# One pool of eight PSUM banks, two turned parts of q and k, and a new order, in a post-norm decoder layer

## The reference

```python
x = layernorm(x + self_attention(x))   # 16 heads of 32; q, k rms-normalised over 512 and rotated; causal
x = layernorm(x + xattn(x, ctx, ctx))  # 8 "heads" of 16 rows: scores are 512x512 over the channels
x = layernorm(x + ffn(x))              # one 512x512 layer, inputs and weight rounded to fp8 blocks of 128

# self_attention
q, k, v = split(h @ Wqkv); q = rope(rmsnorm(q, qw)); k = rope(rmsnorm(k, kw))
o = softmax(causal(q @ k.T / sqrt(32))) @ v @ Wo
# xattn, per head: q, k, v are 16 x 512
ret = softmax(q.T @ k / 4) applied to v
```

## Time and profile before

| | before |
|---|---|
| median of 3 runs | 2888.91 us (2886.74 to 2889.34) |
| the profiled execution, its own time | 2883.74 us |
| its span, first to last instruction | 2882.0 us |
| mean granted clock of PE | 0.987 |
| PE / PEld busy | 2743.4 / 1341.7 us |
| DVE / ACT / POOL busy | 2623.3 / 2233.4 / 1609.2 us |
| DMA | 396.90 MB, 44.6% of 16 engines' span |

### The profile page before, as it was taken

The page is one execution under the profiler, slowest core; times in us unless marked ns, Lnnn a source line. Parts: engine busy times, 40 slices in busy tenths (PEclk is TensorE's granted clock), DMA queues, the critical chain, the costliest instruction groups (busy, mean ns, idle before and its releaser), DMA issues.

```text
span 2882.0 us, 77185 instructions
## 1 busy us (share of the span) xinstructions
PE 2743.4 (95%) x20769; PEld 1341.7 (47%) x20769; DVE 2623.3 (91%) x4038; ACT 2233.4 (77%) x4036; POOL 1609.2 (56%) x2257
## 2 busy tenths in 40 slices
PE   6799999999999999999999999999999999999986
PEld 4544444444444444444444444444444444444421
DVE  7689999999999999999999999999999999998995
ACT  4468788788788788887888887888888888778775
POOL 4446566556556556556556555555555555555543
PEclk8899999999999999999999999999999999999998
DMA  2244444444444444444444444444444444444561
GB/s 100 81 130 151 133 134 136 150 138 135 151 138 134 152 142 130 154 142 127 155 144 131 152 143 128 154 144 134 148 145 131 147 146 137 140 150 126 160 185 51
DMA packets 382299, 396.90 MB, mean 138 GB/s; under 512 B 84369, under 2 KB 313745, under 8 KB 382097
## 3 DMA queue, kind: packets, MB, share of 16 engines
q1 hardware_dynamic: 382096, 394.95, 44.6%
HBM read 208.68 MB, written 186.12 MB: 137 GB/s over the span
## 4 chain that ended last, share of the span: by engine, by line
PE 68%; DVE 19%; issue 7%; ACT 2%; POOL 1%; DMA 1%; SPq 1%; ACTq 0%; DVEq 0%; POOLq 0%
PE bank L1474 18%; PE st L1616 13%; PE pv L1628 12%; PE mx L1602 9%; DVE nm L1314 8%; PE bank L1525 3%; PE bank L1567 2%; DVE yc L1421 2%; PE bank L1467 2%; PE bank L1644 2%; PE bank L1539 2%; PE bank L1645 2%; DVE ropeA L1351 2%; PE bank L1570 1%; ACT pp L1138 1%
## 5 line engine op out<-in xcount | busy, mean ns | idle before, releaser
L1138 ACT ACTIVATE pp<-st 128x512 f32<-128x512 f32 x2048 | 1164.4, 596 | 233.3 <-PE st L1616 220.4
L1314 DVE TENSOR_REDUCE nm<-mx 128x2 f32<-128x1024 f32 x1024 | 1239.0, 1210 | 89.6 <-PE mx L1602 82.1
L1616 PE MATMUL st<-qst,kst 98*128 98x512 f16 x2048 | 738.0, 385 | 23.7 <-ACT pp L1138 21.8
L1628 PE MATMUL pv<-pp,vT 128*17 128x512 f32 x4096 | 537.8, 597 | 0.0
L1602 PE MATMUL mx<-kpair,qpair 64*128 64x512 bf16 x2048 | 399.5, 386 | 44.3 <-DVE nm L1314 36.9
L1474 PE MATMUL bank<-w_h,xT_h 128*128 128x512 f32 x768 | 417.5, 544 | 13.9 <-DVE xT_l L1343 8.1
L1616 PEld LDWEIGHTS st<-qst,kst 98*128 98x128 bf16 x2048 | 179.3, 97 | 401.8 <-issue 202.1
L1602 PEld LDWEIGHTS mx<-kpair,qpair 64*128 64x128 f16 x2048 | 99.0, 92 | 494.0 <-DVE nm L1314 275.6
L1062 POOL TENSOR_SCALAR_AFFINE_SELECT sm<-sm 128x512 f32<-128x512 f32 x256 | 162.8, 636 | 272.9 <-ACT sm L1181 271.3
L1474 PE MATMUL bank<-w_h,xT_l 128*128 128x512 f32 x768 | 307.7, 401 | 0.0
L1474 PE MATMUL bank<-w_l,xT_h 128*128 128x512 f32 x768 | 306.6, 399 | 0.0
(11 more groups left out here) (154 smaller groups left out, 5092.9 us busy)
## 6 DMA issues: line engine op xcount, KB each, us to landing
qst<-q_rows SPq DMA_DIRECT2D x128, 320.0 KB, 3.5
kst<-k_rows SPq DMA_DIRECT2D x128, 320.0 KB, 3.7
kpair<-k_pair_rows SPq DMA_DIRECT2D x256, 128.0 KB, 2.7
qpair<-q_pair_rows SPq DMA_DIRECT2D x256, 128.0 KB, 2.8
k_pair_rows<-kpl SPq DMA_DIRECT2D x64, 384.0 KB, 2.5
q_pair_rows<-qpl SPq DMA_DIRECT2D x64, 384.0 KB, 2.7
q_rows<-qpl SPq DMA_DIRECT2D x64, 384.0 KB, 3.8
k_rows<-kpl SPq DMA_DIRECT2D x64, 384.0 KB, 2.6
```

The lines of the kernel that those rows point to most:

```text
L1138: a.activation(pp[:, unit % 3, j, :], st[n % 2][:], ACT.Exp, scale=CROSS_SCALE).then_inc(st_free, 1)
L1314: v.tensor_reduce(cols, mx[:], AX.X, ALU.max, negate=True).then_inc(mx_free, 1)
L1616: t.matmul(st[n % 2][:], kst[:, h, i * P:(i + 1) * P], qst[:, h, :], start=True, stop=True).then_inc(st_full, 1)
L1628: last = t.matmul(pv[32 * j:32 * j + XD + 1, :], vT[b.i][:, i, GROUPS * j + g, :], pp[:, unit % 3, j, :], start=(i == 0), stop=(i == KC - 1))
```

## The change

PSUM becomes one tensor of eight banks. The table `BANK` gives a bank, and with it a place in that bank's sequence of turns, to every product, also to the 32 `cross_scores_T` (`SC_BANK`), the 16 pairs of `cross_scores` (`MX_BANK`), the two `cross_pv` groups and the turned weights of the fill. `before(name)` now waits on the semaphore of whichever turn held the bank last.

`qkn` has two slots, high and low, for heads i and i + 8 side by side. `part_high` writes one copy. `parts_T` has two steps instead of four, each of 8 transposes of 128 x 128. `self_stack` makes four copies of 64 rows x 1024, from the lower or the upper half of the turned rows, and a new step `copy_part` on SP copies 32 rows of 16 heads x 128 (128 KB) within `qs` and within `ks`; `self_scores:0` waits for both.

All five tables and the fill and drain lists are new. The weights are loaded, rounded and split in six halves, and the memsets of DVE on `qst` and `kst` become a step, `set_rows`, of the fill. The loop's first batch stays number 10.

```diff
-        qkn = [sb(f"qkn{i}", [P, NH, 3, HD], F16) for i in range(2)]
+        qkn = [sb(f"qkn{i}", [P, NH // 2, 2, 2, HD], F16) for i in range(2)]
...
-        st = [bank(f"st{i}") for i in range(2)]
-        pv = bank("pv")
-        mx = es.enter_context(nc.psum_tensor("mx", [P, 2, 512], F32))
-        banks = [bank(f"bank{i}") for i in range(3)]
-        d_w = [sem(f"d_w{i}") for i in range(3)]
+        psum = es.enter_context(nc.psum_tensor("psum", [P, 8, 512], F32))
+        banks = [psum[:, i, :] for i in range(8)]
...
-            ld_x:0@0 ld_kst:1@5 ld_x2r:0@6 ld_sh2:1@5 st_qpair:0@3 ld_qst:1@5 st_sh1:0@1
...
+            st_kpl:0@4 copy_part:0@0 st_qpair:0@2 copy_part:1@0 ld_cx:0@3 ld_qpair:0@3 st_qpl:0@2
...
-            "xT": 2, "tqk0": 0, "tqk1": 0, "tqk2": 1, "tqk3": 2, "q": 2, "k": 1, "v": 2, "s1m0": 1,
-            "s1m1": 0, "s1m2": 1, "s1m3": 1, "s1t0": 0, "s1t1": 0, "s1t2": 1, "s1t3": 1, "pvo": 2,
-            "pvs": 0, "wo": 2, "vT": 0, "xdT": 0, "ffn0": 1, "ffn1": 1, "ffn2": 1, "ffn3": 0}
+            "xT": 2, "tqk0": 6, "tqk1": 3, "q": 2, "k": 0, "v": 3, "s1m0": 3, "s1m1": 6, "s1m2": 7,
+            "s1m3": 3, "s1t0": 7, "s1t1": 4, "s1t2": 4, "s1t3": 3, "pvo": 5, "pvs": 0, "wo": 7, "vT": 5,
+            "pv0": 4, "pv1": 6, "xdT": 3, "ffn0": 6, "ffn1": 4, "ffn2": 1, "ffn3": 3,
+            "wt0": 5, "wt1": 0, "wt2": 4, "wt3": 1, "wpeak": 2}
+        SC_BANK = "47435167657737267272206423421703"
+        MX_BANK = "56 12 12 12 01 56 01 01 01 34 12 01 01 67 45 12"
+        BANK.update({f"sc{n}": int(i) for n, i in enumerate(SC_BANK)})
+        BANK.update({f"mx{q}{n}": int(sorted(pair)[i]) for n, pair in enumerate(MX_BANK.split())
+                     for i, q in enumerate("ab")})
...
+        OWN = {f"sc{n}": (st_free, N_SC, n + 1) for n in range(N_SC)}
+        OWN.update({f"mx{q}{n}": (mx_free, N_MX, n + 1) for n in range(N_MX) for q in "ab"})
+        OWN.update({f"pv{g}": (pv_free, GROUPS, g + 1) for g in range(GROUPS)})
...
+            turns, at = HELD[BANK[name]], AT[name, b.b]
+            if at == 0:
+                return Point(("free", BANK[name]), bank_free[BANK[name]], 0, b, 0)
+            turn, batch = turns[at - 1]
+            assert b.rnd is None or turns[AT[name, b.b + WRAP] - 1] == (turn, batch + WRAP)
+            if turn not in OWN:
+                return nth(turn, bank_free, "free", b, batch)
+            sem, per, n = OWN[turn]
+            return Point((turn[:2], 0), sem, per, b, batch * per + n)
...
+        def part(k, slot):
+            return qkn[k][:, :, :, slot, :].rearrange("p i e d -> p e i d")
+        def both(n):
+            low, high = BANK[f"mxa{n}"], BANK[f"mxb{n}"]
+            return psum[:, low:high + 1:high - low, :]
...
+            def copy_part(b, k):
+                sp.wait_ge(*freed(f"tqk{k}", b))
+                sp.sem_inc(passed_sp, 1)
+                rows = (qs, ks)[k]
+                sp.dma_start(rows[2 * HD:3 * HD], rows[HD * k:HD * (k + 1)]).then_inc(d_copied[k], 16)
...
-                g_.tensor_tensor(qkn[k][:, :, 2 - k, :], ropeA[:].rearrange("p h a d -> p h (a d)"),
-                                 qkn[k][:, :, 0, :], ALU.subtract).then_inc(s_part_l, 1)
+                g_.tensor_tensor(part(k, 1 - k), ropeA[:].rearrange("p (e i) a d -> p e i (a d)", e=2),
+                                 part(k, k), ALU.subtract).then_inc(s_part_l, 1)
...
-                a.activation(w_h[:, :, k * D:(k + 1) * D], pp[:, k], ACT.Copy).then_inc(u_cast, 1)
+                block, half = k // 2, slice(KC // 2 * (k % 2), KC // 2 * (k % 2 + 1))
+                a.activation(w_h[:, half, block * D:(block + 1) * D], pp[:, block, half], ACT.Copy).then_inc(u_cast, 1)
...
-                a.activation(pp[:, unit % 3, j, :], st[n % 2][:], ACT.Exp, scale=CROSS_SCALE).then_inc(st_free, 1)
+                a.activation(pp[:, unit % 3, j, :], at(f"sc{n}"), ACT.Exp, scale=CROSS_SCALE).then_inc(st_free, 1)
...
-                act.wait_ge(*full(f"tqk{2 * k + 1}", b, -1))
-                src = ropeA[:].rearrange("p h a d -> p h (a d)")
-                a.activation(qkn[k][:, :, 0, :], src, ACT.Copy)
-                a.activation(qkn[k][:, :, 1 + k, :], src, ACT.Copy).then_inc(s_part_h, 1)
+                act.wait_ge(*full(f"tqk{k}", b, -1))
+                a.activation(part(k, k), ropeA[:].rearrange("p (e i) a d -> p e i (a d)", e=2), ACT.Copy)\
+                 .then_inc(s_part_h, 1)
...
-                dst = (qs, ks)[i // 2][0:SROWS, 8 * (i % 2):8 * (i % 2) + 8, :]
-                a.activation(dst, at(f"tqk{i}")[0:SROWS, :].bitcast(F16).rearrange("p (h t) -> p h t", h=8), ACT.Copy)\
-                 .then_inc(bank_free[BANK[f"tqk{i}"]], 1)
+                half_rows = slice(2 * HD * (i % 2), 2 * HD * (i % 2 + 1))
+                dst = (qs, ks)[i // 2][0:2 * HD, 8 * (i % 2):8 * (i % 2) + 8, :]
+                copy = a.activation(dst, at(f"tqk{i // 2}")[half_rows, :].bitcast(F16)
+                                    .rearrange("p (h t) -> p h t", h=8), ACT.Copy)
+                if i % 2:
+                    copy.then_inc(bank_free[BANK[f"tqk{i // 2}"]], 1)
...
-            for rows, value in ((qst[64:XROWS, :, :], 0.0), (kst[64:XROWS, :, :], 0.0),
-                                (kst[XROWS:XROWS + 2, :, :], SHIFT_UNIT)):
+            for i in PV_BANKS:
+                v.memset(banks[i], 0.0).then_inc(u_zeroed, 1)
+            def set_rows(b, k):
+                rows, value = ((qst[64:XROWS, :, :], 0.0), (kst[64:XROWS, :, :], 0.0),
+                               (kst[XROWS:XROWS + 2, :, :], SHIFT_UNIT))[k]
+                if k == 2:
+                    dve.wait_ge(u_zeroed, len(PV_BANKS) + 2)
                 v.memset(rows, value).then_inc(u_zeroed, 1)
 
...
-                v.tensor_reduce(cols, mx[:], AX.X, ALU.max, negate=True).then_inc(mx_free, 1)
+                v.tensor_reduce(cols, both(n), AX.X, ALU.max, negate=True).then_inc(mx_free, 1)
...
-                for h in range(8):
-                    last = t.transpose(at(name)[0:SROWS, h * P // 2:(h + 1) * P // 2].bitcast(F16),
-                                       qkn[k][:, 8 * (i % 2) + h, :, :].rearrange("p g d -> p (g d)"), ident16[:])
+                for i in range(NH // 2):
+                    last = t.transpose(at(name)[:, i * P // 2:(i + 1) * P // 2].bitcast(F16),
+                                       qkn[k][:, i].rearrange("p e g d -> p (e g d)"), ident16[:])
...
-                for point in last_of(
-                        freed(f"tqk{c // 2}", b),
-                        freed(f"tqk{2 + c // 2}", b),
-                        before(name, b),
-                ):
-                    pe.wait_ge(*point)
+                if c == 0:
+                    for k in range(2):
+                        pe.wait_ge(d_copied[k], b.n(16, 16))
...
-                pe.wait_ge(mx_free, b.n(N_MX, n))
+                for point in last_of(before(f"mxa{n}", b), before(f"mxb{n}", b)):
+                    pe.wait_ge(*point)
                 for q in range(2):
                     rows = slice(ROW_TILE * q, ROW_TILE * (q + 1))
-                    last = t.matmul(mx[:, q, :], qpair[rows, p, c * P:(c + 1) * P], kpair[rows, p, :],
+                    last = t.matmul(at(f"mx{'ab'[q]}{n}"), qpair[rows, p, c * P:(c + 1) * P], kpair[rows, p, :],
                                     start=True, stop=True)
...
-                pe.wait_ge(st_free, b.n(N_SC, n - 1))
-                t.matmul(st[n % 2][:], kst[:, h, i * P:(i + 1) * P], qst[:, h, :],
+                pe.wait_ge(*before(f"sc{n}", b))
+                t.matmul(at(f"sc{n}"), kst[:, h, i * P:(i + 1) * P], qst[:, h, :],
```

1104 lines of the change are left out of this document (540 added, 564 removed).

## The result

The changed kernel takes **2989.24 us** (median of 4 runs, 2985.50 to 2990.69) where the kernel before takes 2889.07 (4 runs, 2886.74 to 2889.34). The ratio is 1.0348, with a 95% interval of 1.0336 to 1.0361: 100 us slower, far above the forecast of 2802 and outside its range of 2755 to 2852. The profiled execution has a span of 2989.0 us.

What follows compares the result with a forecast made beforehand. PE and DVE were taken to share the bound, DVE alone after the change at 42.1 us a batch. Saving 1.4 us over 57.5 periods (80.5), plus 4 in the fill and 2.5 in the drain, gave 2802 us, range 2755 to 2852.

Steps and rivals of the forecast that it cites:

- worth nothing by itself: ACT, busy 77%: dropping the second copy in `part_high` saves 1.2 us a batch but gains no time alone.
- The period of 43.50 us: Loop: one batch takes 43.50 us, read between two turns of `cx`; 64 batches leave 98 us for filling and draining.
- the floor of DVE: Loop: 43.50 less 1.62 us of waits, so DVE cannot go below 41.9 us a batch with its instructions unchanged.
- Steps 1 and 4: Loop: fewer transposes lower PE's floor to 41.6 us; eight shared banks leave DVE 0.2 of 1.62 us waiting a batch.
- the 1 us by which the prediction called itself wrong: Loop: the prediction counts as wrong if DVE still stands over 1 us a batch.
- The new wait at a bank that another engine holds: Shared banks: such waits can come, as `cross_scores_T:18` for `probs:16`; 0.2 us a batch of DVE waiting left in all.
- Step 3: Two DMA copies before `self_scores:0`: 2.7 us transfer, hidden under PE's work, costed at nothing; bad end 0.7 us of PE.
- Step 6: Fill and drain: 4 us gained as the first projection starts earlier, 2.5 us from fewer waits in the drain.
- The clock: Rival, loop: short stands between products from bank to bank lower PE's clock for a tenth of it; 2981 us, chance 0.02.
- The copies are late: Rival, loop: `self_scores:0` waits for `d_copied` once the chain exceeds 8.5 us; 2946 us at 9.6 us, chance 0.05.

Runs made afterwards that it cites:

- experiment 3: Kernel before with idle ScalarE instructions added at the head of its stream: 2982.49 us with 57 (ratio 1.0326), 2871.83 us with 60 (ratio 0.9946).
- experiment 5: Changed kernel with its loop written out and each of the 16 transposes of q and k issued twice: 2859.45 us, ratio 0.9908.
- experiment 2: The 26 loop turns written out in the same order, no back edge: changed kernel 2834.85 us (ratio 0.9821), kernel before 2851.15 us (ratio 0.9876).

## Why the prediction was wrong, point by point

*The missing term: the loop's back edge.* This is the step that failed. The sum let ACT stand aside (busy 77%, "worth nothing by itself") and had no term for ACT's stand behind the loop's branch and PE's wait for it. It is the largest of all: from the changed kernel to the one with one instruction more, 2989 - 2841 = 149 us. Without it the time is inside the range of 2755 to 2852, though 39 us above the forecast of 2802, and the drain alone is off by more than that. The kernel before pays for its fetch too, 14 us by experiment 3, but nothing in the change's text says that the two pay differently; it is decided by how many ACT instructions stand ahead of the loop and in it, and by how soon PE asks for what ACT's first step frees. The trace of before held a part of this. ACT stood 2.0 us after its branch, and a look at the order of the two tables would have shown that `self_scores:2` now waits for ACT's first step. That ACT would stand twice it did not show.

*The period of 43.50 us.* I took one distance between two turns of `cx` and multiplied by 64. The loop's turn is two batches, and they differ: 43.60 and 42.55 us in the middle. The mean over 52 batches is 43.07. So the floor of DVE by this reckoning was 43.07 - 1.62 = 41.45 us and not 41.9, and filling and draining cost 2882 - 64 x 43.07 = 126 us, not 98. One distance in the longer half was carried through the whole sum.

*Steps 1 and 4, the gain of the loop: near in size, in part by luck.* I forecast 1.4 us a batch; without back edges it is 42.40 - 41.18 = 1.22. PE's own work fell from 1974.30 / 2000 x 42.40 = 41.85 us to 40.63, by 1.22 as well. That is the sum of the 0.90 for the transposes and the 0.3 for fewer changes between products on the whole array and on a part of it that I took for PE; the split was not measured, except that 16 transposes put back added 0.82 of work and only 0.45 of time. Eight transposes take 0.45 us as before (chain of the run with one instruction more, L1541). But I had DVE as the bound with 0.2 us a batch of standing. With one instruction more DVE is busy 1918.64 of 2000 us and so not busy for 1.7 us a batch, over the 1 us by which the prediction called itself wrong, and experiment 5 shows that PE's work sets the pace too. DVE's work did not change (1863.29 / 2000 x 42.40 = 39.50 us a batch, and 39.44, both written out).

*The shared banks.* DVE's wait for POOL's mask (25.8 us) is gone where the loop is undisturbed, and that for the cross scores fell from 48.8 us to 1.9 with one instruction more, as I had forecast (under 10); written out it is 17.6. In the changed kernel it is 21.4 and the other 104.8, both by the back edge. The new wait at a bank that another engine holds, which the prediction allowed for, came on PE: `cross_scores` waits for the bank that `self_norm` on DVE (`o`) reads, 28.1 us or 0.6 a batch, nearly as much as the 32.2 us of PE's two waits before. What the banks alone are worth was not tried. Waits of DVE and of PE with one instruction more:

```profile
DVE nm L1326 <- PE psum L1615: 1.9, 11, 0.2
...
PE psum L1615 <- DVE o L1385: 28.1, 48, 0.7
```

*Step 3, the copies: right in the loop.* No wait of PE for them in the even stretch; the transfer is 2.3 us where I took 2.7. They cost 6 us outside it.

*Step 6, fill and drain.* The 4 us for the fill are right as a sum (x 11 at 431.5 against 436.3), though not for the reason: the first projection starts at 12.89 us where I forecast under 10. The 2.5 us for the drain had the wrong sign and size: it is 50 to 53 us longer. I costed it as a little less waiting and did not ask how many steps are open when the last x goes in. The stages in the tables say that there are more of them. That depth costs time is shown by the added stage (91 us more in the drain) and by the stage taken away (28 less in the drain, with more lost in the fill); how much of the 50 us a better order at the same depth would give back is open, since my own orders moved the fill by 60 us.

*The rivals.* The clock (0.02, 2981 us) came near in its time by luck and was wrong in its mechanism: not short stands from bank to bank but one wait of 4.2 us a turn went ahead of the lower clock, which cost some 2 us a turn, and the granted clock is 1.00 where the wait is gone. "The copies are late" was on the right side by a wait that does not exist. No rival was a wait of ACT for nothing that the profile shows.

## What to carry to other kernels

Before the sum is made, look at each engine's back edge: the gap behind the branch in the chain, the packets on the instruction queues in one turn, and who waits for that engine's first step. Here one instruction ahead of the loop in one engine's stream moved the time by 5% without touching the work; compare such kernels written out, or with a few idle instructions more, before judging the change. Measure a period over many turns, a multiple of the loop's own, and read the depth of a pipeline from its stage numbers, since a stage more was paid here when it drained.

## What the runs showed of the hardware

The instructions of ACT, DVE, POOL and SP come in packets of 8 KB, 128 instructions, on queue 14, and PE's in packets of 16 KB, 256 instructions, on queue 8 (experiment 2). Where ACT's loop body of 328 to 345 instructions lay in three such blocks, the 26 turns fetched nothing (39 or 40 packets a run). Where it touched four, each turn fetched five packets. With the head well inside a block, ACT stood once at the branch, 2.0 us in the kernel before and 2.3 with 64 instructions more; with the head one or two instructions ahead of a border it stood twice, 4.6 and 4.1 us together. The Trainium skill's section named above gives blocks of 16 KiB and 256 instructions; that agrees with queue 8, but the packets of queue 14 here are half of that, and the measurement decides.

The other engines had their next instruction 0.3 us or less after each branch back to the head, PE with 1414 instructions a turn included.

Where PE waited 4.2 us a turn, the granted clock fell to 0.50 (1.2 GHz) once a turn, and eight products took 1.84 us for 0.98; with the 64 instructions and a wait of 1.9 us it fell in 10 of the 23 turns from 500 to 2500 us, and where the wait was gone it was 1.00 throughout.
